# Indexer projections in another PSUM bank, and three steps moved in the written-out order of a fused MoE, attention, MoE kernel

## The chip, the cores and the metric

One Trainium2 chip, one of its cores. The metric is device time in microseconds of one execution; lower is better. Times are medians over runs. The profile is of one execution, so its span (first to last instruction) is a little shorter than the device time of that same execution.

## The reference

Eight sequences of 256 tokens with 256 features pass three residual steps: half of a mixture-of-experts feed-forward, a sparse attention, and half of the same feed-forward again. The attention step is where the change lies:

```
x = layernorm(x)
qi = hadamard((x @ wq_idx).reshape(B, S, 16, 128))      # indexer queries
ki = hadamard(x @ wk_idx)
I  = sum over heads of iw * relu(qi . ki)               # index scores, causal
idx = top_k(I, 32)
q, k, v = x @ wq, x @ wk, x @ wv                        # 16 query heads, one k and v
p = softmax(q . k[idx] * 128 ** -0.5)
o = (p @ v[idx]) @ wo
```

## The kernel before

The 2048 tokens are four groups (g = 0 to 3) of 512 tokens, two sequences each. One generator, `order()`, writes out all steps of the kernel as tuples. Each engine walks the whole list and issues its own part of each step, in that order. So the list is the program order of every engine's queue. Engines wait for each other only through semaphores.

Nearly every product is split into a high and a low float part (fp32r), so a 512-column projection is six matmuls, and its result has to be taken out of PSUM ("drained") by ScalarE (a copy of the high part) and then by VectorE (subtraction, which gives the low part). VectorE's last read raises the bank's semaphore. `banks(st)` says which of the eight PSUM banks a step writes. Before TensorE begins a step it calls `free(bank)`, which waits until every earlier step of that bank in the list has been drained.

The steps that matter here:

- `("qi", g, h)`: indexer query projection of head h. ScalarE makes two copies of it and VectorE one subtraction. `("q", n)`: the attention query projection, the same shape. n is 16 g + h.
- `("l", g, h)`: indexer products with the keys into banks 1 and 2; ScalarE applies relu and VectorE accumulates into I.
- `("scores", U)`, U = 0 to 63: attention products of unit U, into banks 1 and 2. VectorE adds the mask and reduces, ScalarE applies exp, `("scale", U)` takes a reciprocal on VectorE and multiplies on GpSimd.
- `("flip_p", U)`: six transposes of the probabilities, banks 3 and 4. `("pv", U)`: product with the values, bank 5; drained by ScalarE (copy into OH, 512 columns) and VectorE (subtraction into OL, 512 columns). `("wo", U)`: output projection.
- `("values", g)`: projection of the values of a group, banks 3 and 4, drained in two rounds that alternate between ScalarE and VectorE through one buffer R, which `l` uses too.
- `("half", "m1", g, i, bank)`: four transposes of normalised rows for the second feed-forward, drained by ScalarE and VectorE with 512 columns each.
- `best` and `mask`: the search for the 32 largest index scores, on VectorE alone. `drip(1)` yields one of these steps at a time. While U is under 32 it does so after `scale`, and skips u = 7, 11 and a few others (u = U mod 16).

With U under 32 a unit of the list reads: `qi`, `scores(U)`, `wo(U-3)`, `l`, `q`, `scale(U)`, one `best` or `mask` step (VectorE), `pv(U-2)`, `flip_p(U-1)`, and then the next unit's `qi`. Before the change, for groups 2 and 3 `qi` and `q` write bank 0 (but for three `qi` and the first three `q`), and bank 5 is `pv`'s.

The bank wait that the change works through is this one, at the head of each TensorE step:

```python
def free(bank):
    t.wait_ge(S[f"bank{bank}"], n.get(("bank", bank), 0))
    t.wait_ge(S["xres"], n.get(("emptied", bank), 0))
```

Of the kernel before, what the change touches and what calls it, by code (L numbers as in the profile page):

```python
# [30 lines left out]
def order():  # L31

    def bring(*names):
        return [("bring", q) for q in names]
# [14 lines left out]
    def centre(key, g, at, *engines):  # L49
        k = 4 // len(engines)  # L50
        return [("centre", key, g, at, eng, k * i, k) for i, eng in enumerate(engines)]

    def part(n, q):
        return ("ex", n, q // 2, q % 2)

    def scatters(n, *groups):
        return [st for r in range(2) for g in groups for st in
                [("tag", n, g)] * r + [("scatter", n, i, r) for i in range(4 * g, 4 * g + 4)]]

    def marks(n, *groups):  # L60
        return [("mark", n, g, 0) for g in groups]
# [88 lines left out]
    def weigh(name):  # L150
        return bring(name) + split("pool", "pool", name)
# [46 lines left out]
    def begin_topk(g):  # L198
        left.extend((what, g, b, r) for b in range(2) for what, r in [("best", r) for r in range(4)] + [("mask", 0)])
        return [("causal", g, 0), ("causal", g, 1)]  # L200

    def drip(k):
        out = left[:k]
        del left[:k]
        return out
# [3 lines left out]
    def ahead_to(U):  # L209
        while nextq[0] <= min(U, 63):  # L210
            yield ("q", nextq[0])
            nextq[0] += 1
# [17 lines left out]
    yield from ahead_to(0)  # L230
    yield from [("project", 0, 2), ("iw", 2), ("qi", 2, 0)]
    yield from ahead_to(1)
    yield from [("values", 0), ("l", 2, 0), ("qi", 2, 1)]

    later = scatters(1, 0, 1)

    def prepare(U):

        stats = lambda g, i: [("stats", "m1", 4 * g + 2 * i, 2, 4 * g + 2 * i)]
        rest = lambda g, p: [(p, "m1", 4 * g, 4, 4 * g)]  # L240
        half = lambda g, i: [("half", "m1", g, i, 1 + i)]
        first, second, third = [], [], []
        for i, U0 in enumerate((20, 21, 35, 37, 51, 52)):
            if U == U0:
                first += stats(i // 2, i % 2)
        for i, U0 in enumerate((22, 39, 52)):
            if U == U0:
                first += rest(i, "rough")
        for i, U0 in enumerate((23, 41, 53)):
            if U == U0:  # L250
                first += rest(i, "moments")
        for g, begin in ((0, 24), (1, 42), (2, 53)):
            if U in (begin, begin + 1):
                third += centre("m1", g, 4 * g, "act", "act")[U - begin:U - begin + 1]
        for i, U0 in enumerate((34, 36, 44, 45, 55, 55)):
            if U == U0:
                second += half(i // 2, i % 2)
        for g, U0 in enumerate((46, 46, 56)):
            if U == U0:
                first.append(("logits", 1, g, 0 if g == 1 else 5))  # L260
        for q, begin in ((0, 47), (1, 57)):
            if U == begin:
                first.append(("pick", 1, q))
            elif U == begin + 1:
                first.append(("sel", 1, q))
            elif U == begin + 2:
                first += [("shift", 1, q), ("count", 1, q, 5), ("place", 1, q, 5)]
            elif U == begin + 3:
                first += [("choose", 1, q)] + (marks(1, 2) if q else marks(1, 0, 1))
                if q:  # L270
                    later.extend(scatters(1, 2))
        if U == 31:
            third.append(("blank", 1))
        elif 32 <= U < 40:
            third += [("clear", k) for k in (2 * U - 64, 2 * U - 63) if k < CLEARS]
        elif U == 62:
            third += bring(*(part(1, q) for q in range(6)))
        if U >= 50:
            third += later[:2]
            del later[:2]  # L280
        for i in range(3):
            if U == 32 + i:
                third += bring(("sh", 1, i))
            elif U == (50, 52, 58)[i]:
                third.append(("hi", ("sh", 1, i), "act"))
            elif U == (54, 56, 61)[i]:
                first.append(("lo", ("sh", 1, i), "dve"))
        return first, second, third

    for U in range(64):  # L290
        g, u = divmod(U, 16)
        gi, hi = divmod(U + 34, 16)
        idx = gi < NG
        first, second, third = prepare(U)
        if 0 < u < 14 and idx:
            yield ("qi", gi, hi)
        elif idx and (u == 15 or U == 16):
            yield ("qi", gi, hi - 1)
        yield ("scores", U)
        if U >= 32 and not first:  # L300
            yield from drip(1)
        yield from first
        if u == 15 and g + 1 < NG:
            yield ("project", 1, g + 1)
        if u == 14 and g < 2:
            yield ("flip", "q", g + 1, 3, 4)
        if U == 13:
            yield ("flip", "a", 3, 3, 4)
        if U >= 3:
            yield ("wo", U - 3)  # L310
        if u == 1 and U > 1:
            yield from [("pv", U - 2), ("values", g)]
        if U == 0:
            yield from ahead_to(2)
        if idx:
            if u == 14:
                yield from [("project", 0, gi), ("iw", gi)]
            elif u == 15:
                yield ("l", gi, 0)
            elif u == 0:  # L320
                yield from [("l", gi, 1), ("qi", gi, 2)]
            else:
                yield ("l", gi, hi)
        if 0 < u < 14 and U < 32 or u == 15 or U in (32, 33, 49):
            yield from ahead_to(U + 2 if U < 33 else U + 3)
        yield ("scale", U)
        if U < 32 and u < 13 and u != 1 and (u == 3 or u % 4 != 3):
            yield from drip(1)
        if U >= 2 and u != 1:
            yield ("pv", U - 2)  # L330
        yield from second
        if U:
            yield ("flip_p", U - 1)
        yield from ahead_to(U + 2 if U < 32 else U + 3)
        if idx and u == 0:
            yield ("l", gi, 2)
        if U < 3:
            yield from weigh(("wo", 3 + U))
        elif U < 5:
            yield from weigh(("wq", 3 + U))  # L340
        elif U < 7:
            yield from weigh(("wo", 1 + U))
        if U == 8:
            yield from centre("a", 3, 12, "act")
        if u == 10 and g < 2:
            yield from centre("q", g + 1, 4 * g + 4, "act")
        if u == 13 and g < 2:
            yield from begin_topk(g + 2)
        yield from third
# [63 lines left out]
def task(st):  # L413

    n, g, i = st[1:4]
    return 3 * ((0, 1, 3, 2), (0, 1, 2, 3))[n][g] + i


def banks(st):

    kind = st[0]
    if kind == "flip":
        return st[3:5]
    if kind == "half":
        return (st[4],)
    if kind in ("logits", "unturn"):
        return (st[3],)
    if kind == "count":
        return (st[3],)
    if kind == "offs":  # L430
        return (st[2],)
    if kind == "gu":
        c = task(st)
        return (c % 2, 2 + c % 2)
    if kind in ("turn_x", "hidden", "turn_g", "sink"):
        return ({"turn_x": 0, "hidden": 2, "turn_g": 4, "sink": 6}[kind] + st[2] % 2,)
    if kind == "project":
        return ((3 if st[2] < 3 else 0, 0 if st[2] < 2 else 5)[st[1]],)
    if kind == "q":
        return (5 if st[1] < 3 else 0,)  # L440
    if kind == "qi":
        return ((0, 5)[st[2] % 2] if st[1] < 2 else 5 if st[1:] in ((2, 4), (3, 0), (3, 4)) else 0,)
    if kind in ("l", "scores"):
        return (1, 2)
    if kind == "iw":
        return (1,)
    if kind in ("values", "flip_p"):
        return (3, 4)
    if kind == "pv":
        return (5,)  # L450
    return ()
# [46 lines left out]
def macaron_kernel(nc, x, cst_in, row_in, gw_in, wsh_in, wex_in, wqi_in, ws_in, wiw_in, wq_in, wo_in, out):  # L498
# [7 lines left out]
    AX = mybir.AxisListType  # L506

    stages = list(order())
    at, whole = tally(stages)
    ctx = ExitStack()  # L510
    with ctx:
# [218 lines left out]
        for st in stages:  # L730
            if st[0] in ("flip", "half"):
                TURNS.setdefault(st[1:3], []).extend((st, bank) for bank in banks(st))
# [42 lines left out]
        def _(e):  # L775
# [33 lines left out]
            for st in stages:  # L809
# [141 lines left out]
                elif kind == "project":  # L951
# [5 lines left out]
                    w = weight(("sm", which))[2]  # L957
                    H, L = SLOTS[slot(key, g)]
                    bank = banks(st)[0]
                    free(bank)  # L960
                    pairs = [(w[:, 128 * dc:128 * dc + 128], w[:, 256 + 128 * dc:384 + 128 * dc],
# [977 lines left out]
```

## Time and profile before

| | us |
|---|---|
| three runs | 954.46, 955.21, 956.78 |
| median | 955.21 |
| the profiled execution | 956.78 |
| its span | 954.8 |
| TensorE busy in the span | 894.0 (94%) |
| VectorE busy | 694.8 (73%) |
| ScalarE busy | 552.4 (58%) |
| granted TensorE clock, mean | 0.973 |

Attention runs from about 200 to 792 us of the span. Units U = 0 to 31, in which `qi` and `l` of groups 2 and 3 are woven into the attention of groups 0 and 1, lie between about 312 and 577 us. In the profile all drains by ScalarE's copy carry line L1071 (the helper `copy`), all VectorE subtractions line L1261 (the helper `tt`), and all matmuls L782 (`three`) or L787 (`plain`). What an instruction belongs to is told by its tiles and its place in time.

### The profile page before, as it was taken

Reading aid. Unit: us, or ns where it says so; the run is one execution under the profiler, and the core shown is the slowest. Engines: PE = TensorE matmul, PEld = TensorE weight load, DVE = VectorE, ACT = ScalarE, POOL = GpSimd, SP = SyncE. Lnnn points to the kernel's source line nnn. Section 1 sums busy time; section 2 is a strip of 40 time slices with the busy share of each in tenths; the row PEclk is TensorE's granted clock in tenths of the full one; section 3 lists DMA queues with packets and bytes.
Section 4 is the critical chain, followed back from the end, with each engine's and each line's share of the span. In section 5 each row is a group of like instructions: output and inputs, shape, how many; then the busy total and the mean of one; then the engine's idle time right before and its main releaser. Section 6 shows DMA issues by size and latency. Waiting matters only on the chain.

```text
span 954.8 us, 19123 instructions
## 1 busy us (share of the span) xinstructions
PE 894.0 (94%) x5847; PEld 797.4 (84%) x5847; DVE 694.8 (73%) x2380; ACT 552.4 (58%) x1590; POOL 434.7 (46%) x569
## 2 busy tenths in 40 slices
PE   7786999899999899999999999999999998989987
PEld 3466999787778799899899998999999986779986
DVE  7884777569797677775788767878587766767756
ACT  4553554345655666766566766667468664545543
POOL 0682787342400465333233343555258780226652
PEclk9996999999999999999999999999899999889989
DMA  9233545461100010000000004991001134024455
GB/s 351 92 120 91 160 145 162 88 118 43 46 12 1 17 40 2 1 1 2 1 1 1 2 1 136 316 319 41 1 13 44 37 112 143 29 78 134 135 192 178
DMA packets 52451, 81.32 MB, mean 85 GB/s; under 512 B 5824, under 2 KB 37184, under 8 KB 52352
## 3 DMA queue, kind: packets, MB, share of 16 engines
q1 hardware_dynamic: 44672, 58.26, 19.9%
q0 software_dynamic: 7680, 21.83, 7.4%
q8 instruction: 50, 0.82, 0.4%
q14 instruction: 49, 0.40, 0.2%
HBM read 40.01 MB, written 40.06 MB: 84 GB/s over the span
## 4 chain that ended last, share of the span: by engine, by line
PE 69%; DVE 11%; ACT 6%; issue 6%; POOL 5%; DMA 2%; SPq 0%; DVEq 0%; POOLq 0%; ACTq 0%
PE ps L782 34%; PE ps L787 28%; PE ps L1028 4%; POOL xg L1751 3%; DVE RR L1261 2%; ACT RR L1071 2%; PE ps L910 1%; PE ps L937 1%; DMA FA<-xg 1%; DVE PA L1636 1%; DVE st L1302 1%; PE ps L825 1%; DMA yr<-FA,IDX 1%; POOL yr L1765 1%; DVE FA L1261 1%
## 5 line engine op out<-in xcount | busy, mean ns | idle before, releaser
L1796 POOL TENSOR_SCALAR SP<-SP,RC 128x128 f32<-128x128 f32 (+1 forms) x256 | 192.6, 769 | 247.7 <-DVE RC L1685 247.5
L1261 DVE TENSOR_TENSOR RR<-ps,RR 128x256 fp32r<-128x256 f32 (+2 forms) x322 | 157.8, 525 | 71.7 <-ACT RR L1071 71.2
L787 PE MATMUL ps<-RR,RA 128*128 (+1 forms) x1002 | 181.6, 322 | 5.9 <-DVE RA L1261 4.5
L787 PEld LDWEIGHTS ps<-RR,RA 128*128 128x128 f32 x1002 | 148.3, 195 | 10.2 <-issue 5.9
L1071 ACT ACTIVATE RR<-ps 128x256 fp32r<-128x256 f32 (+2 forms) x322 | 137.2, 469 | 29.9 <-PE ps L782 27.6
L1230 ACT ACTIVATE SP<-SP,NB 128x128 f32<-128x128 f32 (+1 forms) x256 | 113.5, 444 | 67.2 <-DVE NB L1675 66.9
L782 PE MATMUL ps<-xh,RR 128*128 128x512 f32 x368 | 133.7, 407 | 0.0
L1636 DVE SCALAR_TENSOR_TENSOR PA<-R,IW,PA 128x128 f32<-128x128 f32 x240 | 92.7, 448 | 41.0 <-ACT R L1222 40.8
L1765 POOL DMA_INDIRECT yr<-FA,IDX x78 | 83.7, 1072 | 57.9 <-ACT FA L1071 26.6
L787 PE MATMUL ps<-RR 128*128 128x256 f32 x768 | 103.9, 285 | 2.3 <-DVE RR L1261 2.2
L787 PEld LDWEIGHTS ps<-RR 128*128 128x128 f32 x768 | 97.1, 192 | 3.4 <-DVE RR L1261 3.0
L782 PE MATMUL ps<-xh,RT 128*128 128x512 f32 x272 | 97.2, 404 | 0.3 <-DVE RR L1261 0.3
L782 PEld LDWEIGHTS ps<-xh,RR 128*128 128x128 f32 x368 | 70.0, 190 | 13.5 <-DVE RR L1261 0.2
L1261 DVE TENSOR_TENSOR RA<-ps,RA 128x256 fp32r<-128x256 f32 x156 | 65.1, 419 | 21.0 <-ACT RA L1071 20.8
L1071 ACT ACTIVATE RA<-ps 128x256 fp32r<-128x256 f32 x156 | 59.8, 384 | 27.6 <-PE ps L910 26.5
L782 PE MATMUL ps<-KH,RR 128*128 128x256 f32 x256 | 75.5, 323 | 0.0
L782 PE MATMUL ps<-KIH,RR 128*128 128x256 f32 x256 | 75.4, 323 | 0.0
L1071 ACT ACTIVATE QF<-ps 128x256 f32<-128x256 f32 x96 | 36.9, 384 | 64.1 <-PE ps L782 64.1
L782 PE MATMUL ps<-xl,RR 128*128 128x512 f32 x184 | 73.2, 398 | 0.0
L1222 ACT ACTIVATE R<-ps 128x384 f32<-128x384 f32 x128 | 58.7, 482 | 20.9 <-DVE PA L1636 8.0
L782 PE MATMUL ps<-RR,VH 128*128 128x512 f32 (+1 forms) x256 | 66.4, 341 | 0.1
L782 PEld LDWEIGHTS ps<-xh,RT 128*128 128x128 f32 x272 | 51.6, 190 | 10.4 <-DVE RR L1261 0.5
(236 smaller groups left out, 1928.8 us busy)
## 6 DMA issues: line engine op xcount, KB each, us to landing
xg<-stage SPq DMA_DIRECT2D x15, 1161.0 KB, 14.1
FA<-xg SPq DMA_DIRECT2D x78, 129.0 KB, 2.1
RAW<-wex_in SPq DMA_DIRECT2D x16, 352.0 KB, 6.8
RAW<-wex_in SPq DMA_DIRECT2D x16, 256.0 KB, 6.8
X<-yr POOLq DMA_DIRECT2D x6, 512.0 KB, 5.4
RAW<-yr SPq DMA_DIRECT2D x6, 512.0 KB, 6.0
RAW<-wsh_in SPq DMA_DIRECT2D x6, 384.0 KB, 7.6
X<-x_in SPq DMA_DIRECT2D x4, 512.0 KB, 4.8
```

The lines of the kernel that those rows point to most:

```text
L782: ins = e.matmul(o, a, c, start=first and i == 0, stop=last and i == len(seq) - 1, skip_group_check=True)
L787: return e.matmul(o, a, c, start=start, stop=stop, skip_group_check=True)
L825: ins = e.transpose(PS[bank][:, 128 * i:128 * i + 128], src[:, i, 128 * dc:128 * dc + 128], ident[:])
L1028: ins = e.transpose(PS[3 + i][:, 128 * z:128 * z + 128], SP[:, k, i, 128 * z:128 * z + 128], ident[:])
L1071: return e.activation(o, i, ACT.Copy)
L1222: e.activation(R[:, b, :], PS[1 + b][:, 0:384], ACT.Relu).then_inc(S[f"bank{1 + b}"], 1)
L1230: ins = e.activation(SP[:, k, i, o:o + w], SP[:, k, i, o:o + w], ACT.Exp, scale=-1.0, bias=NB[:, k, 2 * i + z:2 * i + z + 1], accum_out=SM ...
L1261: return e.tensor_tensor(o, p, q, alu)
L1636: ins = e.scalar_tensor_tensor(Is, r, iw, Is, ALU.mult, ALU.add)
L1751: e.indirect_dma_start(out=XG[m], out_offset=bass.IndirectOffsetOnAxis(ap=XI[:, r, i:i + 1], axis=0), in_=NORMED[buffer(f"m{m}", g)][:, i ...
L1765: e.indirect_dma_start(out=YR[m], out_offset=bass.IndirectOffsetOnAxis(ap=IDX[:, j % 8:j % 8 + 1], axis=0), in_=MOE[m].YS[:, j % 4, :], in ...
L1796: ins = e.tensor_scalar(SP[:, k, i, o:o + w], SP[:, k, i, o:o + w], RC[:, k, 2 * i + z:2 * i + z + 1], None, ALU.mult)
```

## The change

Three edits in the list and one in `banks`:

- `qi` of groups 2 and 3 is put in bank 5 instead of bank 0, but for (2,0), (2,1), (2,2) and (3,2), which stay in bank 0. (2,4), (3,0) and (3,4) were in bank 5 already. This moves 23 of the steps to a place directly behind `pv` and `flip_p`, and two more: (2,3), and (3,3), which comes behind `q(18)` and `l(3,2)`.
- `values(0)` moves from before `l(2,0)` to unit 0, behind `scale(0)` and the `best` step, before `l(2,2)`.
- The two `half` steps of m1's group 0 move from units 34 and 36 to units 33 and 34.

```diff
@@ order()
-    yield from [("values", 0), ("l", 2, 0), ("qi", 2, 1)]
+    yield from [("l", 2, 0), ("qi", 2, 1)]
...
-        for i, U0 in enumerate((34, 36, 44, 45, 55, 55)):
+        for i, U0 in enumerate((33, 34, 44, 45, 55, 55)):
             if U == U0:
                 second += half(i // 2, i % 2)
...
         yield ("scale", U)
         if U < 32 and u < 13 and u != 1 and (u == 3 or u % 4 != 3):
             yield from drip(1)
+        if U == 0:
+            yield ("values", 0)
         if U >= 2 and u != 1:
             yield ("pv", U - 2)
@@ banks(st)
     if kind == "qi":
-        return ((0, 5)[st[2] % 2] if st[1] < 2 else 5 if st[1:] in ((2, 4), (3, 0), (3, 4)) else 0,)
+        return ((0, 5)[st[2] % 2] if st[1] < 2 else 0 if st[2] == 2 or st[1:] in ((2, 0), (2, 1)) else 5,)
```

## Rows read from the trace of the kernel before

**Rows 1.** The page's part 2: TensorE's granted clock in 40 slices, tenths.
```profile
PEclk9996999999999999999999999999899999889989
```

**Rows 2.** TensorE's waits, 342:566 (waited for: us in total, times, longest).
```profile
PE ps L787 <- DVE NB L1675: 1.3, 3, 0.4
```

**Rows 3.** Timeline, one unit with `best` (start us, us, engine, line, op, tiles).
```profile
340.99 0.39 PE L782 MATMUL ps<-xh,RR 128*128 128x512 f32 x1
...
342.11 0.43 DVE L1261 TENSOR_TENSOR RR<-ps,RR 128x256 fp32r<-128x256 f32 x1 [0.30 <-ACT RR L1071]
342.15 0.28 PE L782 MATMUL ps<-RR,VL 128*128 128x256 f32 x1
...
342.28 0.82 PE L1028 MATMUL ps<-ident,SP 128*128 128x128 f32 x6
...
342.47 0.60 ACT L1071 ACTIVATE RR<-ps 128x512 fp32r<-128x512 f32 x1 [0.40 <-PE ps L782]
...
342.85 0.48 PE L782 MATMUL ps<-xh,RT 128*128 128x512 f32 x1
...
343.50 0.41 DVE L1653 MATCH_REPLACE8 W<-M,W 128x256 f32<-128x256 f32 x1
343.83 0.68 DVE L1261 TENSOR_TENSOR RR<-ps,RR 128x512 fp32r<-128x512 f32 x1
```

**Rows 4.** Timeline, one unit without `best` or `mask`.
```profile
375.76 0.48 PE L782 MATMUL ps<-xh,RT 128*128 128x512 f32 x1
376.02 0.69 DVE L1261 TENSOR_TENSOR RR<-ps,RR 128x512 fp32r<-128x512 f32 x1 [0.48 <-ACT RR L1071]
```

**Rows 5.** Timeline, one unit with `mask`.
```profile
359.30 0.48 PE L782 MATMUL ps<-xh,RT 128*128 128x512 f32 x1
...
360.64 0.68 DVE L1261 TENSOR_TENSOR RR<-ps,RR 128x512 fp32r<-128x512 f32 x1
```

**Rows 6.** Timeline around `qi(3,3)`.
```profile
457.27 1.34 DVE L1261 TENSOR_TENSOR RR<-ps,RR 128x384 fp32r<-128x384 f32 x3
...
458.67 0.50 PE L782 MATMUL ps<-xh,RT 128*128 128x512 f32 x1 [0.29 <-DVE RR L1261]
```

**Rows 7.** Timeline after `centre` in unit 8, and at the next `l`.
```profile
384.85 2.08 ACT L1107 ACTIVATE xn<-X,nt 128x256 f32<-128x256 f32 x4
...
388.63 0.46 PE L787 MATMUL ps<-PA 128*128 128x128 f32 x2 [0.44 <-DVE NB L1675]
```

**Rows 8.** Timeline around `values(0)`, `scores(0)`, `l(2,2)` and `l(2,3)`.
```profile
308.62 0.42 DVE L1261 TENSOR_TENSOR R<-R,ps 128x256 f32<-128x256 f32 x1 [0.24 <-ACT R L1071]
...
311.64 0.87 ACT L1222 ACTIVATE R<-ps 128x384 f32<-128x384 f32 x2 [1.33 <-DVE VL L1261]
...
312.28 0.46 PE L787 MATMUL ps<-KF,QF 128*128 128x128 f32 x2 [0.61 <-ACT R L1222]
...
319.03 0.46 PE L787 MATMUL ps<-PA 128*128 128x128 f32 x2 [1.41 <-ACT PA L1071]
...
319.90 0.41 DVE L1653 MATCH_REPLACE8 W<-M,PA 128x256 f32<-128x256 f32 x1
...
320.41 1.69 DVE L1636 SCALAR_TENSOR_TENSOR PA<-R,IW,PA 128x128 f32<-128x128 f32 x4
...
323.66 0.46 PE L787 MATMUL ps<-PA 128*128 128x128 f32 x2 [0.69 <-DVE NB L1675]
```

**Rows 9.** Timeline, unit 33 and `scores(34)`; the last row: a `half` drain.
```profile
598.51 0.39 PE L787 MATMUL ps<-KF,QF 128*128 128x128 f32 x2
...
598.77 0.42 DVE L1261 TENSOR_TENSOR RR<-ps,RR 128x256 fp32r<-128x256 f32 x1
...
603.78 0.68 DVE L1261 TENSOR_TENSOR RT<-ps,RT 128x512 fp32r<-128x512 f32 x1
```

**Rows 10.** Timeline: a long wait in the last stage; windows: busy, PEclk after it.
```profile
828.63 1.61 PE L787 MATMUL ps<-RT,RA 128*128 128x256 f32 x8 [2.30 <-DVE RA L1261]
...
829.20:832.60 3.40, 3.40 (x14) 3.02 (x13) 2.68 (x4) 2.38 (x4) 0.47 (x2) 0.50 0.14 44
```

## The prediction

> **What bounds the kernel now.** I read the page first: TensorE is busy 94% of the span (table above), and its granted clock is full or nearly so through the attention (from the ninth of the 40 slices to the 33rd, with one 8) [rows 1]. Then TensorE's waits in the stretch where the change acts. In 224 us its largest entry is 1.3 us in three waits [rows 2]. So TensorE is the bound there, back to back, and every microsecond that it is made to wait is added to the time. Nothing can be won in this stretch beyond those waits; the question is what the new bank order makes TensorE wait for. That is read from the timeline of one unit [rows 3]: when does each bank come free, and how far behind is the step that would now need it?
>
> **Part 1, `qi` in bank 5.** Before, `qi` shares bank 0 with `q`. The last matmul of `q` starts at 340.99, and VectorE's subtraction that frees bank 0 ends at 342.11 + 0.43 = 342.54. The first matmul of the next `qi` starts at 342.85 [rows 3]. The bank is free 0.31 us early and nobody waits.
>
> After, `qi` shares bank 5 with `pv`, which stands only one short step ahead of it: `pv`'s last matmul starts at 342.15, six transposes of `flip_p` follow, then `qi` [rows 3]. The bank is free only when ScalarE has made OH (342.47, 0.60 us) and VectorE has made OL. OL runs from 343.83 to 344.51. `qi` would start at 342.85, so it is 1.66 us too early for its bank.
>
> Could OL come earlier once TensorE waits? It is held from both sides by TensorE itself. OH starts right behind `pv`, after ScalarE has been idle for 0.40 us. On VectorE, the subtraction of `q` comes after an idle 0.30 us, then reciprocal and the `best` step, which ends at 343.50 + 0.41 = 343.91 (overlapped by the start of OL) [rows 3]. Neither engine is behind with old work: both wait for TensorE in the same unit. If TensorE is later, they are later by the same amount. The 1.66 us therefore comes back in every such unit.
>
> The unit without a `best` or `mask` step: OL ends at 376.02 + 0.69 = 376.71, `qi` starts at 375.76, 0.95 us apart [rows 4]. With `mask`: 360.64 + 0.68 = 361.32 against 359.30, 2.02 us [rows 5].
>
> How many: a `qi` that comes directly behind `pv` and `flip_p` and is now in bank 5 is (2,5) to (2,15), (3,1), and (3,5) to (3,15): 11 + 1 + 11 = 23. By the rule for `drip`, 14 of them follow a `best` step, 4 a `mask`, and 5 neither. So 14 x 1.66 + 4 x 2.02 + 5 x 0.95 = 23.2 + 8.1 + 4.8 = 36.1 us. Handing over costs a little more: at `qi(3,3)` VectorE's drain ends at 457.27 + 1.34 = 458.61 and TensorE starts at 458.67, 0.06 us later [rows 6]. 23 x 0.06 = 1.4 us. Together 37.5 us. The lower bound of this part is 23 x 1.01 = 23.2 us, if `best` and `mask` somehow got out of OL's way. The upper is 23 x 2.08 = 47.8 us, if every unit behaved as the one with `mask`.
>
> Behind the waiting `qi` stand `scores`, `wo`, `l`, `q` and `pv` of the unit, all of TensorE's queue. ScalarE and VectorE then starve too; GpSimd's multiplication has a whole unit of room.
>
> What the waits give back. `qi(3,3)` waits 0.29 us for bank 0 before [rows 6] and has bank 5 to itself after: -0.3 us. The three waits of 1.3 us [rows 2] come in the units with a `centre`: its 2.08 us on ScalarE push back `qi`'s copies, VectorE's reduction, and with it `l` [rows 7]. After the change `centre` runs while TensorE stands still. It ends at 386.93, and `qi`, moved to about 385.7, would not need ScalarE before about 387.3 (six matmuls at the spacing of some 0.23 us, as between `q`'s last and `pv`'s first, and the 0.4 us until a copy starts). So all three go: -1.3 us.
>
> **Part 2, `values(0)` later.** Removed ahead of `l(2,0)`: 16 matmuls, 1.9 us, and behind them the wait of `scores(0)`, 0.61 us [rows 8], which came because relu needs R, held until 311.64 by the rounds of `values`. With the pipeline's refill TensorE reaches `l(2,1)` 2.7 us earlier. In the new place the 1.9 us of matmuls fill the idle time before `l(2,2)`, 1.41 us [rows 8], so `l(2,2)` is still some 2.4 us early. But VectorE reaches `values` only behind the `best` step, whose end moves from 320.31 to about 317.7. From there the two rounds take what they took before, from 308.62 to the relu at 311.64, 3.0 us. That puts the relu of `l(2,2)` at 320.7. `scores(1)` follows 0.64 us behind it (312.28 against 311.64), at 321.4, where it would have arrived at 319.3: a new wait of 2.1 us. Then VectorE has, from 0.5 us behind the relu, `l`'s accumulations (1.69), `qi`'s subtraction (0.4, as [rows 3]) and the first half of the reduction of `scores(1)` (0.7, an estimate) before `l(2,3)` may start: 324.0, against 323.66 before [rows 8]. Net +0.3 us. The bounds are -2.7 us (the 2.7 us early are kept) and +2.1 us (the new wait is paid in full and nothing is kept). I take +0.3, since each link has its own row.
>
> **Part 3, `half` earlier.** The matmuls only move. But in unit 33 `half` (bank 1) is followed by `flip_p(32)` and then at once by `scores(34)`, which needs bank 1; there is no `q` between them. `scores(34)` starts at 598.51 before [rows 9]; with four more transposes in front (0.45 us) it would arrive at 598.96. VectorE is behind in this unit because of `values(2)`: the subtraction of `q(36)` ends at 599.19 [rows 9], the reciprocal takes 0.1, `half`'s subtraction 0.68 (as at 603.78 [rows 9]). Bank 1 is free at 599.97: a wait of 1.1 us. The second `half`, now in bank 2 in unit 34, has the distance that the first had there. Bounds 0 and +2 us; I take +1.1.
>
> **The sum.** 37.5 - 0.3 - 1.3 + 0.3 + 1.1 = 37.3 us. The profiled span of 954.8 us becomes 992.1, and that execution's 956.8 becomes 994.1. The median of the three runs lies 1.6 us lower, at 955.2, so I forecast 992.5 us.
>
> **The rivals.**
>
> A, a queue that catches up (not slower). If OL were late only because ScalarE and VectorE lag behind a fast TensorE, the first wait would let them catch up and the rest would be free. One wait of 1.7 us is paid, the 1.6 us of old waits go, and `values(0)` may keep its 2.7 us: 955.2 + 1.7 - 1.6 - 2.7 = 952.6 us. This decides if OL can end within the 0.70 us between `pv`'s last matmul and `qi`. Against it: OH and OL alone take 0.60 + 0.68 us, and both engines were idle just before [rows 3]. Chance 3%.
>
> B, VectorE's `best` and `mask` cost no delay, for instance because they move into the new idle time. Then each unit costs 1.01 us: 23.2 in place of 37.5, so 978.2 us. Against it: they stand between `q`'s subtraction and OL in VectorE's own order, and `q` comes late with TensorE. Chance 7%.
>
> C, the clock. TensorE's granted clock falls to its lower level (1.2 GHz) after some waits: the 2.30 us before 828.63 are followed by 3.4 us at 0.50 [rows 10]. In such a stretch TensorE, busy throughout, loses 1.7 us. If the new waits set that off in each of the 23 units, it costs 39 us more: 1031 us; in one of four, about 10 more: 1002. Against it: the 1.41 us of idling before 319.03 [rows 8] left the clock at 9 (90% or more) in that slice, the 14th, and in the next ones [rows 1]; the new waits are of that size, but come every 10 us and just behind transposes. Chance 8% for a dip in at least one unit of four.
>
> The Trainium skill ("TensorE: Matmul & The Clock Gate", section "A second HAM failure mode: psum-queue depth-cycling") speaks for C: cycling through PSUM banks can leave short idle spells between groups of matmuls, and the clock then swings between its two levels. By that rule the time would be up to C's; by the row at 319.03 it would be the forecast. The trace so far does not bear the rule out for waits of this length.
>
> **How the numbers follow.** The forecast has 81%, A 3%, B 7%, C 8%, and 1% is left for the change making no difference. The forecast's own range is 984 to 1001: the bounds of parts 2 and 3 (-4 to +3) and a tenth of part 1 (about 4) to each side. Taking in B and the mild form of C, the range is 978 to 1003. A measurement of this kernel tells 0.3% (3 us) from no change. Faster by more than that: 0.03. Within it: 0.02. Slower: 0.95.
>
> **What would show it.** TensorE's waits between 330 and 610 should hold about 23 entries on VectorE's subtraction, some 1.6 us each by their mean, and a unit should take 9.9 us (9.2 without a `best` step) where it took 8.23: four units lie between the `qi` of 342.85 and that of 375.76 [rows 3, 4]. VectorE's subtraction of 512 columns should end just before each `qi`. The idle time before `l` in the units with `centre` should be gone. `scores(1)` should show a wait of about 2 us, `l(2,2)` none, and `scores(34)` one of about 1 us. The forecast is wrong if units keep 8.2 us (A), if they take 9.2 us throughout (B), or if PEclk shows 7s and 8s in slices 14 to 24 (C).

## The result and the profile after

The median of four runs is 995.5 us (993.2 to 997.8) against 954.8 us before (four runs too, the three of the table and one more): 4.3% slower, ratio 1.0426 with a 95% interval of 1.039 to 1.046. The forecast was 992.5 us in a range of 978 to 1003. The profiled execution took 995.8 us, its span is 993.8 us, 39.0 us longer than before.

The page after, parts 1 and 2 (busy us; the granted clock in slices now 24.8 us wide), in answer to the table and to [rows 1]:

```profile
PE 901.0 (91%) x5847; PEld 798.3 (80%) x5847; DVE 698.0 (70%) x2380; ACT 553.0 (56%) x1590; POOL 433.7 (44%) x569
PEclk9979999999999899999999999999999999999999
```

Of the slices in which `qi` and `l` are woven in (the 14th to the 25th), one shows less than 9: the 14th (323 to 348 us), with 8.

TensorE's waits between 330 and 615 us, in answer to [rows 2] (line numbers are two higher than before, so L1263 is the helper that was L1261):

```profile
PE ps L784 <- DVE RR L1263: 31.7, 23, 1.8
PE ps L789 <- DVE NB L1677: 0.7, 1, 0.7
PE ps L827 <- DVE RR L1263: 0.3, 2, 0.2
```

These are the 23 waits that were counted from the list. A `best` unit, in answer to [rows 3] (timeline: start, duration, engine, line, op, tiles):

```profile
348.22 0.42 DVE L1263 TENSOR_TENSOR RR<-ps,RR 128x256 fp32r<-128x256 f32 x1 [0.44 <-ACT RR L1073]
348.26 0.28 PE L784 MATMUL ps<-RR,VL 128*128 128x256 f32 x1
348.38 0.82 PE L1030 MATMUL ps<-ident,SP 128*128 128x128 f32 x6
...
348.58 1.36 ACT L1073 ACTIVATE RR<-ps 128x512 fp32r<-128x512 f32 x3 [0.40 <-PE ps L784]
...
349.60 0.41 DVE L1655 MATCH_REPLACE8 W<-M,W 128x256 f32<-128x256 f32 x1
349.93 1.61 DVE L1263 TENSOR_TENSOR RR<-ps,RR 128x512 fp32r<-128x512 f32 x3
350.67 0.50 PE L784 MATMUL ps<-xh,RT 128*128 128x512 f32 x1 [1.47 <-DVE RR L1263]
```

OL starts 1.67 us behind `pv`'s last matmul (349.93 against 348.26); before it was 1.68 us. The chain has moved as one piece, and nothing has caught up. TensorE resumes 0.06 us after OL's 0.68 us. The idle time shown, 1.47 us, is less than the 1.74 us by which the unit grows, since it counts from the modelled end of the last transpose. From this `qi` (350.67) to the next (360.63) it is 9.96 us, where 9.9 were expected. A unit without a search step, and one with `mask`, in answer to [rows 4, 5]:

```profile
391.72 0.50 PE L784 MATMUL ps<-xh,RT 128*128 128x512 f32 x1 [0.76 <-DVE RR L1263]
370.95 0.50 PE L784 MATMUL ps<-xh,RT 128*128 128x512 f32 x1 [1.82 <-DVE RR L1263]
```

What answers to [rows 8] is where the forecast was off. The timeline of `values(0)`'s second round, of GpSimd beside it, and of `scores(1)` and `l(2,3)`:

```profile
320.11 0.54 DVE L1601 CAST VH<-R 128x256 fp32r<-128x256 f32 x1
320.58 1.26 POOL L1734 TENSOR_TENSOR RR<-stage,RR 128x512 fp32r<-128x512 f32 x1
320.68 1.45 DVE L1263 TENSOR_TENSOR VL<-R,VH 128x256 fp32r<-128x256 f32 x1
...
322.76 0.49 PE L789 MATMUL ps<-KF,QF 128*128 128x128 f32 x2 [3.31 <-ACT R L1224]
...
325.18 0.77 PE L789 MATMUL ps<-PA 128*128 128x128 f32 x2 [1.00 <-DVE NB L1677]
```

The wait of `scores(1)` is 3.31 us, not 2.1. And TensorE's clock fell behind it, and twice more between two waits further on (windows: us, then busy time of PE, PEld, DVE, ACT, POOL, PEclk, DMA):

```profile
324.54:331.37 6.83, 6.19 (x23) 5.53 (x24) 2.97 (x14) 3.84 (x13) 0.00 (x0) 0.50 0.01 4
372.33:375.74 3.41, 3.41 (x18) 3.31 (x17) 1.66 (x9) 1.80 (x7) 1.54 (x2) 0.50 0.00 0
532.75:536.16 3.41, 3.41 (x11) 2.85 (x11) 0.79 (x3) 0.66 (x2) 0.86 (x1) 0.50 0.00 0
```

### The profile page after: what moved, and what is told of

Same layout as the page of the kernel before. It is cut to its first block, busy times and chain, and to the rows that moved or that the text cites. A ratio compares the mean times of both kernels' runs of the same rounds, so it can differ in the third digit from the quotient of the medians.

```text
span 993.8 us, 19116 instructions
## 1 busy us (share of the span) xinstructions
PE 901.0 (91%) x5847; PEld 798.3 (80%) x5847; DVE 698.0 (70%) x2380; ACT 553.0 (56%) x1590; POOL 433.7 (44%) x569
## 4 chain that ended last, share of the span: by engine, by line
PE 65%; DVE 18%; ACT 6%; issue 6%; DMA 2%; another core or an unknown queue 1%; POOL 0%; SPq 0%; DVEq 0%; POOLq 0%; ACTq 0%
PE ps L784 31%; PE ps L789 28%; DVE RR L1263 4%; PE ps L1030 2%; ACT RR L1073 2%; DVE PA L1638 2%; PE ps L939 2%; PE ps L912 1%; ACT SP L1232 1%; DVE st L1304 1%; DVE FA L1263 1%; DVE M L1652 1%; DVE PA L1263 1%; PE ps L827 1%
## 5 line engine op out<-in xcount | busy, mean ns | idle before, releaser
L1263 DVE TENSOR_TENSOR RR<-ps,RR 128x256 fp32r<-128x256 f32 (+2 forms) x322 | 159.3, 527 | 109.8 <-ACT RR L1073 108.9
L1263 DVE TENSOR_TENSOR RA<-ps,RA 128x256 fp32r<-128x256 f32 x156 | 65.1, 420 | 12.9 <-ACT RA L1073 7.8
```

The source lines that it names most:

```text
L1263: return e.tensor_tensor(o, p, q, alu)
```

## The experiments

In what follows a "delay" is the difference between the start of one step's last matmul in the variant's trace and in the trace before, less the same difference just ahead of the stretch in question. It takes out what happened earlier in the execution. For the four kernels that were run once, only these delays are read and not the times (953.7, 962.9, 954.7 and 967.4 us in their order below, against 953.1): at 300 us, ahead of every moved step, their traces are already -1.9, 6.2, -0.4 and 8.6 us off the trace before. Ratios are against the kernel before on the same chip.

**The bank edit alone**, `banks` changed as in the diff, the list as before. Expected:

> The kernel before with the bank edit alone. Theory 1 (each of the 23 qi waits for the drain of the pv just ahead of it, and the drain comes late with TensorE, so nothing is caught up): 23 waits that lengthen the units by 37.9 us in all, less 2.0 us of old waits at l in the centre units and 0.5 us at qi(3,3): +35.4 us, ratio about 1.037, about 990 us. Theory 2 (the bank costs less and the rest of the 41 us came from the moved values step and the clock): at most +30 us. Rival A (the queues catch up after the first wait): about 955 us.

Measured: 988.6 us against 952.7, ratio 1.037 (1.032 to 1.041). TensorE's waits between 305 and 610 us:

```profile
PE ps L782 <- DVE RR L1261: 31.7, 23, 1.8
PE ps L787 <- ACT PA L1071: 1.4, 1, 1.4
```

The same 31.7 us in 23 waits. The delay from `pv(0)` to `scores(32)` is 37.0 us; one fall of the clock in it (3.4 us at 0.50) costs 1.6, which leaves 35.4. Theory 1 holds to the tenth; theory 2 and rival A fall.

**Without the bank edit**, that is `values(0)` and `half` moved alone. Expected:

> The changed kernel with qi of groups 2 and 3 back in its old bank, so only values(0) and the two half steps are moved. Theory 1: no wait of about 1.7 us in the units from 2 to 28; the time is what the two moves cost in the changed kernel's trace, 1.1 us for half and 2 to 4.3 us for values (4.3 if the clock falls again behind the long wait of scores(1)): 958 to 960 us. Theory 2: over 965 us.

Measured: 958.4 us against 952.7, ratio 1.0055 (1.003 to 1.008). No wait of the new kind is left; between 330 and 560 us the trace has:

```profile
PE ps L789 <- DVE NB L1677: 2.0, 4, 0.7
```

The trace before has the same entry in this stretch: the three waits of the `centre` units, and one of 0.7 us at `l(2,4)`. With the run before, this splits the change: 3.7% for the bank, 0.5% for the two moves.

**The search steps behind `pv`**, on top of the bank edit:

```diff
-        if U < 32 and u < 13 and u != 1 and (u == 3 or u % 4 != 3):
-            yield from drip(1)
         if U >= 2 and u != 1:
             yield ("pv", U - 2)
+        if U < 32 and u < 13 and u != 1 and (u == 3 or u % 4 != 3):
+            yield from drip(1)
```

> The bank edit alone, and each best or mask step of units 0 to 31 moved behind pv in the list, so that VectorE does OL before it. The work is the same. Theory 1 (the drain's place in VectorE's order makes the wait): every one of the 23 waits is as in a unit without such a step, 1.0 us instead of 1.74 (14 of them) and 2.09 (4): 14 x 0.72 + 4 x 1.07 = 14.4 us less than the bank edit alone, about 976 us. Rival (VectorE's amount of work per unit makes the unit long): no change against the bank edit alone, about 990 us.

Measured: 972.6 us, ratio 1.021 (1.018 to 1.023), so 16.0 us less than the bank edit alone, for the same work. A `mask` unit in the timeline, and the waits between 305 and 610 us:

```profile
425.56 0.28 PE L782 MATMUL ps<-RR,VL 128*128 128x256 f32 x1
...
426.51 0.69 DVE L1261 TENSOR_TENSOR RR<-ps,RR 128x512 fp32r<-128x512 f32 x1 [0.48 <-ACT RR L1071]
427.12 0.65 DVE L1264 TENSOR_SCALAR W<-W 128x128 f32<-128x128 f32 x2
427.26 0.51 PE L782 MATMUL ps<-xh,RR 128*128 128x512 f32 x1 [0.76 <-DVE RR L1261]
```
```profile
PE ps L782 <- DVE RR L1261: 17.4, 23, 0.8
```

OL now comes right behind OH, `mask` behind OL, and all 23 waits have the length of a unit without a search step. From `pv(0)` to `scores(32)` the delay is 21.3 us; the expectation was 23 x 1.0 less 2.5. So the order on VectorE makes 14.1 us of the loss by the traces (35.4 less 21.3) and 16.0 by the times; its amount of work is the same in both.

**Six matmuls between bank and reuse**, on top of the last:

```diff
-        if 0 < u < 14 and U < 32 or u == 15 or U in (32, 33, 49):
+        if u == 15 or U in (32, 33, 49):
             yield from ahead_to(U + 2 if U < 33 else U + 3)
```

`q(U+2)` then comes from the later `ahead_to`, behind `flip_p`.

> As the last, and q of units under 32 also moved behind flip_p, so that six matmuls of 512 columns (1.28 us) stand between pv's bank 5 and the qi that reuses it; qi is in bank 5 in all 23 places. Theory 1 (distance to the last user of the bank decides, not which bank it is): the waits of about 1 us are covered by 1.28 us, none is left, 954 to 957 us. Rival (a bank shared with pv costs as such, or the unit's chain of drains stays too long): waits of half a us and more in most units, 965 us and above.

Measured: 957.3 us, ratio 1.0048 (1.003 to 1.007). The waits between 305 and 610 us:

```profile
PE ps L787 <- issue: 3.0, 6, 0.7
PE ps L787 <- DVE NB L1675: 2.5, 5, 0.7
PE ps L787 <- ACT PA L1071: 1.4, 1, 1.4
PE ps L782 <- DVE RR L1261: 0.8, 1, 0.8
```

Of the 23 waits for bank 5 one is left (0.8 us, `qi(3,1)`, where `q(17)` still stands ahead of `pv`). `qi` is in bank 5 in all 23 places, so sharing it with `pv` costs nothing by itself; the distance does it. The time lies 0.3 us above the 954 to 957 us that were expected. What is left over the kernel before is in part a new wait: `scores(U)` of an even U needs `q(U+1)`, which now comes so late that TensorE waits for its drain (the six put down to "issue"). In unit 6:

```profile
361.70 0.74 DVE L1261 TENSOR_TENSOR RR<-ps,RR 128x256 fp32r<-128x256 f32 x2
...
362.21 0.46 PE L787 MATMUL ps<-KF,QF 128*128 128x128 f32 x2 [0.49 <-issue]
```

**`half` alone** (34 and 36 become 33 and 34). Expected:

> The kernel before with the two half steps of m1's group 0 moved alone. Theory 1: scores(34) waits about 1.1 us for bank 1 (VectorE's subtraction of half), nothing else changes: +1.1 us in the trace from unit 34 on. Rival: the wait is hidden, because q(36) and values(2) are drained sooner than reckoned: 0.

Measured, one run: the delay behind unit 36 is 1.07 us, and between 598 and 606 us there is one wait:

```profile
PE ps L787 <- DVE RT L1261: 1.1, 1, 1.1
```

**`values(0)` alone.** Expected:

> The kernel before with values(0) moved alone. Theory 1: as in the changed kernel, scores(1) waits about 3.3 us for relu, and l(2,3) starts about 2 us later than before; if the granted clock falls behind that wait again, q(3) and flip_p(0) add about 2 us more. Rival (the excess of 1.7 us over the 0.3 us that I forecast came from the bank edit in the same stretch): l(2,3) starts within 0.5 us of before.

Measured, one run: `scores(1)` waits 3.3 us again, `l(2,3)` is 2.1 us late, `pv(0)` 4.2 us. The clock fell again, for 6.8 us from 330.3. So this loss is not the bank's.

```profile
PE ps L789 <- ACT R L1224: 3.3, 1, 3.3
PE ps L789 <- DVE NB L1677: 0.9, 1, 0.9
```

**`values(0)` ahead of the search step:**

```diff
         yield ("scale", U)
+        if U == 0:
+            yield ("values", 0)
         if U < 32 and u < 13 and u != 1 and (u == 3 or u % 4 != 3):
             yield from drip(1)
-        if U == 0:
-            yield ("values", 0)
```

> As the last, but values(0) ahead of the best step in unit 0, so VectorE drains it first. Theory 1 (VectorE's order): the wait of scores(1) falls by about 1.3 us, to about 2.0, but the best step then stands ahead of the accumulations, so l(2,3) starts as late as with values behind best: its own wait grows by as much. On the clock: if the length of one wait decides, it does not fall here. Rival (the two rounds of values themselves are the cost, wherever they stand): the wait of scores(1) stays at 3 us or more.

Measured, one run. Waits of TensorE between 305 and 332 us:

```profile
PE ps L789 <- DVE NB L1677: 2.0, 1, 2.0
PE ps L789 <- ACT R L1224: 1.0, 1, 1.0
```

The wait of `scores(1)` fell by 2.3 us (1.3 were expected) and that of `l(2,3)` rose by 1.1. `l(2,3)` is 0.8 us late, `pv(0)` 2.9 us. VectorE's second round was over here before GpSimd's subtraction began (320.09), so the extra 1.0 us (and the 1.3 at `l(2,3)`) fit the next experiment. On the clock I was wrong: it fell here too (6.8 us at 0.50 from 322.2), with no wait over 2.0 us.

**GpSimd's weight split out of unit 0**, on top of `values(0)` alone:

```diff
         if U < 3:
-            yield from weigh(("wo", 3 + U))
+            for k in ((), (3, 4), (5,))[U]:
+                yield from weigh(("wo", k))
```

> As values(0) moved alone, and GpSimd's split of the weight wo 3 moved from unit 0 to unit 1. In the changed kernel's trace one subtraction of values (VL from R and VH, all in SBUF) took 1.45 us while GpSimd ran its own subtraction, where it takes 0.43 us else. Theory 1 (the two engines hinder each other on SBUF): the subtraction is 0.43 us again and scores(1) starts 1.0 us earlier, its wait 2.3 us. Rival (a long record by chance, or for another reason): it stays near 1.4 us.

Measured, one run. The second round on VectorE in `values(0)` alone, then here:

```profile
326.46 0.54 DVE L1601 CAST VH<-R 128x256 fp32r<-128x256 f32 x1
327.03 1.45 DVE L1263 TENSOR_TENSOR VL<-R,VH 128x256 fp32r<-128x256 f32 x1
```
```profile
328.86 0.29 DVE L1602 CAST VH<-R 128x256 fp32r<-128x256 f32 x1
329.19 0.42 DVE L1264 TENSOR_TENSOR VL<-R,VH 128x256 fp32r<-128x256 f32 x1
```

The wait of `scores(1)` is 2.0 us instead of 3.3 (2.3 were expected), and `l(2,3)` is 0.8 us late instead of 2.1. Theory 1 holds: 1.3 us of the miss were VectorE beside GpSimd, 1.0 in the subtraction and 0.25 in the cast ahead of it. As a kernel it is no better: a new wait of 0.8 us appears before `qi(2,5)`.

**`values(0)` in unit 1**, right behind `scores(1)`, and then **`q(3)` into unit 0** as well (`ahead_to(3)` behind `qi(2,2)`, in bank 5), on the kernel before:

> The kernel before with values(0) moved to unit 1, between scores(1) and l(2,3). Theory 1 (matmuls put into an idle stretch of TensorE cost nothing, and their drain costs nothing if the next user of R's reader is far enough): scores(0) keeps the 0.6 to 0.9 us that the move wins everywhere, the 1.9 us of matmuls fill the 0.7 us wait of l(2,3), and the rounds with ScalarE and VectorE end before scores(2) needs relu of l(2,3): about 1.7 us less in the trace by pv(0). Rival (as in unit 0, the rounds hold up relu and then scores): no gain or a loss of 1 to 2 us. In the times either is 0.2%.

> As the last, and q(3) moved from unit 1 into unit 0 between qi(2,2) and l(2,2), in bank 5, so that 1.28 us of matmuls stand in the 1.41 us wait of l(2,2) for the drain of qi(2,2). Theory 1: another 1.2 us less by pv(0), about 3 us in all, 0.3% less time than before. Rival (q(3)'s copies on ScalarE then delay relu of l(2,2) and with it scores(1) by as much): nothing more than the last.

Measured: ratios 1.0020 (0.999 to 1.005) and 0.9986 (0.996 to 1.001), 12 runs each; neither can be told from before. In the first, the delay by `pv(0)` is 1.9 us where -1.7 was expected; the clock falls in it once, for 3.4 us. In the second it is 0.2 where about -3 was expected, without a fall. Theory 1 falls in both. The waits of the second between 305 and 345 us show why:

```profile
PE ps L791 <- DVE NB L1679: 1.7, 1, 1.7
PE ps L1032 <- DVE R L1265: 1.6, 2, 1.1
```

`l(2,2)` starts at once now, but `flip_p(0)` waits for banks 3 and 4, which `values` has just filled, and `l(2,4)` for a VectorE that is behind. The matmuls could be put into the idle time; their drains could not.

## Why the prediction was right, and which term was off

The delays along the trace, from step to step:

| step of the prediction | forecast | measured |
|---|---|---|
| 23 waits of `qi` for bank 5 | 37.5 | 37.9 |
| old waits in the `centre` units | -1.3 | -2.0 |
| `qi(3,3)` in its own bank | -0.3 | -0.5 |
| `values(0)` in unit 0 | +0.3 | +4.5 |
| `half` in unit 33 | +1.1 | +1.1 |
| clock, two falls in units 2 to 28 | 0 (rival C) | +3.1 |
| the rest of the execution | 0 | -5.1 |
| sum (span) | 37.3 | 39.0 |

- **Part 1 was right in place, count and price.** Each of the 23 waits has the size read from before: 1.74 (1.66 + 0.06 forecast) with `best`, 2.09 with `mask`, 1.02 with neither. That one could read them there rested on one observation: in [rows 3] both draining engines were idle just before their part, so the chain hangs on TensorE itself.
- **The waits given back** were taken from the idle time that the waits' view shows (0.44 us each); measured by the steps they were 0.66 us each. The idle time counts from a modelled end and leaves out the slower first matmul behind a wait (the second follows it by 0.34 us, the later ones by 0.23: 350.67, 351.01, 351.24).
- **Part 2 is the term that was mis-sized**: "From there the two rounds take what they took before, 3.0 us". They took 4.5 us, from 317.74 to the relu at 322.22, and 1.3 of the 1.5 us more go when GpSimd's weight split is moved away from them. So `l(2,3)` began 1.6 us late instead of 0.3. The other 2.9 us come between there and `pv(0)`, with the clock: it fell while `l(2,3)` and `q(3)` ran, in the changed kernel and in every variant with `values(0)` in unit 0. I had looked for that only behind the 23 waits.
- **Part 3** was right to the tenth.
- **Rival A** fell with the bank edit alone. **Rival B** was wrong as a forecast, but its price is real: with the search steps behind OL, each wait is about 1.0 us. **Rival C** came true in a weak form. The 8 in the 14th slice is one of its signs, but stems from `values(0)`. Behind the 23 waits there are two falls in the changed kernel, one with the bank edit alone, and none in the variant whose 23 waits are about 1 us. All three begin 0.2 to 1.4 us behind the wait of a `mask` unit, the longest kind (the one that ends at 370.95 stands ahead of the fall at 372.33). That is three of the eight `mask` waits in the two traces and none of the 38 shorter ones. Each fall costs 1.6 us.
- **The rest**, -5.1 us, is behind unit 36. Along the traces it comes in three places: -1.6 us from 673 us of the trace before, -1.7 from 843, -2.2 from 915, and +0.4 elsewhere. In each place the clock was low for longer before: 6.8 us each time, against 3.4 us, none, and 3.4 us after. The windows of these falls, three before and then two after:

```profile
672.20:679.00 6.80, 6.80 (x31) 6.51 (x31) 0.47 (x3) 0.27 (x1) 2.98 (x4) 0.50 0.01 2
842.80:849.60 6.80, 5.91 (x27) 5.26 (x26) 2.88 (x5) 2.12 (x5) 2.08 (x4) 0.51 0.44 113
914.60:921.40 6.80, 5.92 (x22) 5.45 (x23) 2.43 (x7) 1.86 (x5) 1.72 (x3) 0.50 0.24 73
```
```profile
717.10:720.50 3.40, 3.40 (x16) 3.21 (x16) 0.47 (x3) 0.00 (x0) 2.75 (x4) 0.50 0.00 0
956.00:959.40 3.40, 3.24 (x13) 3.19 (x13) 1.49 (x5) 0.89 (x3) 0.00 (x0) 0.50 0.17 63
```

The trace of the bank edit alone bears it out: it lacks the first fall, and its delay shrinks by 3.2 us there; in the third place its clock is low for 6.8 us too, and its delay stays. (The -2.2 us are 0.5 more than 3.4 us at half speed can take; that part stays open.) These falls differ between kernels whose steps there are the same (the third lasts 3.4 us with `half` alone), so I don't put them down to the change.

- **Luck in the total.** The span came out 1.7 us above the forecast (993.8 against 992.1). Behind that stand 7.3 us of loss that the sum did not have (4.2 in part 2, 3.1 of clock behind the waits) and 5.1 us less in later stages, where the clock fell for shorter times. Part 1, nine tenths of the sum, was no luck. Also, the forecast's own range should have ended at 999.5 us by its terms (992.5 + 3 + 4), not at 1001.

The Trainium skill ("TensorE: Matmul & The Clock Gate", section "A second HAM failure mode: psum-queue depth-cycling") describes a kernel whose clock swings between its two levels under short idle spells from cycling through PSUM banks. The traces here agree only in part: three falls behind 46 waits.

## What to carry to other kernels

A PSUM bank is free only when its last reader in the engines' own order is done. So before you give a bank a second user, measure in the trace the time from the last user's final matmul to the end of its drain (2.4 us here with a `best` step in between, 1.6 us without), and compare it with the matmul time that stands between the two users (0.7 us here; in its old bank `qi` had 1.9 us, for a drain of 1.6). If the draining engines are idle before their part, the difference is paid every time, and it shrinks by moving other work behind the drain or matmuls in front of the reuse. Then look for who needed the matmuls that you moved.

## What was not expected of the hardware

VectorE's subtraction with two SBUF inputs took 1.45 us beside GpSimd's subtraction of 1.26 us (which reads SBUF too), and 0.42 us without it. The Trainium skill states this ("SBUF — State Buffer", section "SBUF: two separate sides"): VectorE and GpSimd share one pair of ports, an operation holds it for its whole length, and a VectorE operation with two SBUF inputs needs it against a GpSimd operation that reads SBUF. The trace agrees: the subtraction began 0.10 us behind GpSimd's and ended 0.29 us behind its end. In the first round it began 0.09 us ahead of GpSimd's next operation, and was not slowed:

```profile
318.72 0.43 DVE L1263 TENSOR_TENSOR VL<-R,VH 128x256 fp32r<-128x256 f32 x1
318.81 1.13 POOL L1798 TENSOR_SCALAR SP<-SP,RC 128x256 f32<-128x256 f32 x1
```

VectorE's cast, with one SBUF input, took 0.33 to 0.54 us beside GpSimd in these traces and 0.29 us alone; what held it was not tested by itself. What this would have shown for the forecast: a step on VectorE that is moved may land beside a GpSimd step, and then its duration read in the old place does not hold.

The clock fell to its lower level (1.2 GHz) for 6.8 us in all five traces with `values(0)` in unit 0. The two waits around the beginning of the fall were 3.3 and 0.9 to 1.0 us in three of them, 2.0 and 0.8 in one, and 1.0 and 2.0 in one. So in this stretch it needed no wait longer than 2.0 us. Why a wait of 1.8 us sets it off in three cases of eight, these runs don't tell.
